# Last layer of a four-layer image kernel: the recurrent state of a pair of images is loaded in seven parts, one per chunk of the pair before, in place of four transfers at once

## What is computed

```python
x = x + _L0_conv_ref(_gn(x), ...)          # attention
x = x + _L1_conv_ref(_gn(x), ...)          # deformable convolution
x = x + _L2_conv_ref(_gn(x), ...)          # diagonal LSTM, left and right
x = x + _L3_conv_ref(_gn(x), ...)          # deformable convolution, adaptive
...
def _diag_lstm(x, w_i2s, b_i2s, w_ih, b_ih, b_hh, k0, k1, b_s2s):
    ...
    _, hs = jax.lax.scan(step, (z, z), xs)            # wd = 2 * w - 1 = 111 steps
    outs = hs.reshape(wd, b, COUT, h).transpose(1, 2, 3, 0)
    return _unshift(outs, w)
left = _diag_lstm(x, *params)
right = jnp.flip(_diag_lstm(jnp.flip(x, 3), *params), 3)
right = jnp.concatenate([jnp.zeros_like(right[:, :, :1, :]), right[:, :, :-1, :]], axis=2)
return left + right
```

## Time and profile before

| | us |
|---|---|
| Median of 3 runs, not profiled | 12763.94 (12756.97 to 12778.16) |
| Span of the profiled execution | 13258.5 |
| POOL busy, of that span | 7518.9 (57%) |
| PE busy | 7451.2 (56%) |
| DVE busy | 6180.1 (47%) |
| Last layer in the profile | 7942 to the end, some 5317 |

### The profile page before, as it was taken

One profiled execution on the slowest core, in us unless ns is written; L12 is line 12 of the kernel. 1 busy time (PEld: TensorE's weight loads), 2 busy tenths in 40 slices (PEclk: granted clock), 3 DMA queues, 4 the chain that ended last, 5 costly groups with the idle time before them and its releaser, 6 DMA issues. The chain is left out here.

```text
span 13258.5 us, 114790 instructions
## 1 busy us (share of the span) xinstructions
PE 7451.2 (56%) x29878; PEld 2708.4 (20%) x29878; DVE 6180.1 (47%) x8631; ACT 4757.6 (36%) x7391; POOL 7518.9 (57%) x7857
## 2 busy tenths in 40 slices
PE   7786776778777676853289992333232323233332
PEld 2222222222222222221123321111111111111111
DVE  1344444444433444445456664454455445545444
ACT  7664554646555454641156661111111111111100
POOL 0375655657565564757500004777777767767776
PEclk9897887889888787876599995565565656555665
DMA  0232232223322222337633337343434343433332
GB/s 9 66 96 87 85 93 80 87 89 96 92 85 79 89 85 86 91 94 172 164 86 81 82 78 139 101 121 101 120 97 119 101 111 98 120 97 101 100 96 90
DMA packets 1169072, 1280.23 MB, mean 97 GB/s; under 512 B 795966, under 2 KB 924414, under 8 KB 1164670
## 3 DMA queue, kind: packets, MB, share of 16 engines
q0 software_dynamic: 338688, 925.30, 23.5%
q1 hardware_dynamic: 815710, 347.84, 11.1%
q10 hardware_dynamic: 14368, 3.21, 0.1%
HBM read 1080.00 MB, written 195.82 MB: 96 GB/s over the span
## 5 line engine op out<-in xcount | busy, mean ns | idle before, releaser
L423 POOL DMA_INDIRECT b_gathered<-table,b_iu x3528 | 3701.6, 1049 | 1929.9 <-issue 1013.0
L423 POOL DMA_INDIRECT d_gathered<-table,d_iu x3528 | 3705.2, 1050 | 1420.4 <-issue 1041.0
L526 PE MATMUL PS<-ident,d_sample 128*128 128x128 f32 (+1 forms) x1960 | 509.6, 424 | 2978.1 <-DVE d_sample L879 2090.9
L504 PE MATMUL PS<-b_key 64*128 64x448 f32 (+1 forms) x5600 | 1516.6, 622 | 448.9 <-ACT b_weights L665 300.1
L665 ACT ACTIVATE b_weights<-PS 128x896 f32<-128x896 f32 (+1 forms) x1400 | 1270.1, 907 | 1287.5 <-remote 882.8
L861 DVE TENSOR_TENSOR d_gathered<-d_gathered,PS 128x2304 f32<-128x2304 f32 x392 | 1000.9, 2553 | 1184.1 <-DMA d_gathered<-table,d_iu 1115.1
L514 PE MATMUL PS<-b_weights,b_values 128*64 128x448 f32 (+1 forms) x5600 | 1462.9, 603 | 123.1 <-issue 73.4
L668 ACT ACTIVATE b_weights<-b_weights 128x896 f32<-128x896 f32 (+1 forms) x1400 | 1332.3, 952 | 44.7
L674 ACT ACTIVATE d_sampleT<-PS 128x512 f32<-128x512 f32 x392 | 233.6, 596 | 2894.4 <-PE PS L526 2000.9
L526 PEld LDWEIGHTS PS<-ident,d_sample 128*128 128x128 f32 (+1 forms) x1960 | 336.0, 205 | 3130.8 <-issue 2721.1
L866 DVE TENSOR_TENSOR b_gathered<-b_gathered,PS 128x1152 f32<-128x1152 f32 x392 | 529.9, 1352 | 819.3 <-DMA b_gathered<-table,b_iu 802.6
(11 more groups left out here) (227 smaller groups left out, 9679.5 us busy)
## 6 DMA issues: line engine op xcount, KB each, us to landing
b_gathered<-table,b_iu POOLq DMA_INDIRECT x3528
d_gathered<-table,d_iu POOLq DMA_INDIRECT x3528
l_x_and_h<-xs SPq DMA_DIRECT2D x224, 224.0 KB, 3.9
hs<-l_hT SPq DMA_DIRECT2D x224, 224.0 KB, 2.8
d_h<-hs SPq DMA_DIRECT2D x32, 1554.0 KB
table<-b_table_rows SPq DMA_DIRECT2D x208, 128.0 KB, 2.0
table<-d_table_rows SPq DMA_DIRECT2D x208, 128.0 KB
xs<-b_key SPq DMA_DIRECT2D x14, 1568.0 KB
```

Of the source, the lines that this page charges most:

```text
L423: pool.indirect_dma_start(GB[:, g, k, :], None, tables[b], bass.IndirectOffsetOnAxis(ap=ix, axis=0)).then_inc(gathered[g], 16)
L504: mm = pe.matmul(PS[0:keys(k), 2 * (k % S_BUFS) + a, 0:CH], KEY[r, 0, k * P:k * P + keys(k)], KEY[r, 0, j * CH:(j + 1) * CH], start=True, ...
L526: mm = pe.transpose(PS[0:n, 5 + 2 * (s // 4), (s % 4) * P:(s % 4 + 1) * P], S[:, t % 2, s * P:s * P + n], K.ident[:, :])
```

## The change

The state is cut along its 111 steps into seven parts: six of 16 steps (`H_PART`), one of 15. `load_h_part` issues the four DMAs (direction, image) of one part. `prepare` still loads whole states with `load_h`, which now issues 28 DMAs for one state. In `body` the load no longer stands between the input's load and the first chunk; each chunk issues its own part ahead of its two `write_group` calls, behind the same wait on `h_used`. DVE waits for 64 x 7 increments per pair in place of 64.

```diff
+H_PART = -(-STEPS // NCH)
...
-            def load_h(i):
+            def load_h_part(i, j, last):
+                steps = STEPS - (NCH - 1) * H_PART if last else H_PART
                 for d in (0, 1):
                     for a in (0, 1):
-                        src = hs[1:SLOTS, d, bass.ds((2 * i + a) * H, H), :].rearrange("t r c -> t (r c)")\
-                            .rearrange("t (c r) -> c t r", c=C)
-                        sp.dma_start(HD[a * C:(a + 1) * C, d, :].rearrange("p (t r) -> p t r", r=H), src)\
-                            .then_inc(h_loaded, 16)
+                        src = hs[bass.ds(1 + j * H_PART, steps), d, bass.ds((2 * i + a) * H, H), :]\
+                            .rearrange("t r c -> t (r c)").rearrange("t (c r) -> c t r", c=C)
+                        to = HD[a * C:(a + 1) * C, d, bass.ds(j * (H_PART * H), steps * H)]
+                        sp.dma_start(to.rearrange("p (t r) -> p t r", r=H), src).then_inc(h_loaded, 16)
+
+            def load_h(i):
+                for j in range(NCH):
+                    load_h_part(i, j, j == NCH - 1)
...
                     load(x, n, X[nb])
-                    if not isinstance(n, int):
-                        wait_apart(sp, h_used, n + 1)
-                        load_h(n + 1)
...
                     elif nxt:
+                        if not isinstance(n, int):
+                            wait_apart(sp, h_used, n + 1)
+                            load_h_part(n + 1, j, last)
                         write_group(n, nb, 2 * j, 0)
...
-                    v.wait_ge(h_loaded, 64 * m + 64)
+                    v.wait_ge(h_loaded, 64 * NCH * (m + 1))
```

## The result

| | median, us | runs | ratio to before, 95% interval |
|---|---|---|---|
| before | 12771.24 (12753.04 to 12780.15) | 20 | |
| changed | 12737.31 (12725.44 to 12749.27) | 20 | 0.9973 (0.9966 to 0.9979) |

The changed kernel is 34 us faster, 0.27%. The forecast time was 12761 with "no difference that can be told" at 0.83 and "faster by over 0.2%" at 0.06; the measured time lies inside the range, but the effect is real, and the sum had given 3 us, at most 6, in that direction.

A forecast was written before the change was run, and what follows sets the result against it. POOL's gather issuing was taken to bound the last layer. A gain of at most 6 us, less 0 to 3 us for small bursts, with SP and start 0, gave 3 us off: 12761 us, range 12730 to 12800.

The forecast's parts named there:

- What bounds the kernel: Last layer: POOL's 3528 gathers, busy and idle ahead, make 5126 of 5317 us, so POOL's issuing sets the pace.
- The burst costs chunk 0 nothing to speak of: Chunk 0 of a pair: the whole-state load costs 1.0 us per pair, so at most 6 us come back.
- rival A: Chunk 0: the state's burst makes it long, so 11.7 us come back six times, 70 us, 12694; chance 0.06.
- Seven small bursts: Each chunk's part delays one block's landing at most 5.5 us, covered by POOL's lead; cost 0 to 3 us.
- a lead of 19.0 us: Last layer: time between a sample's readiness and POOL's earliest need of it, three blocks on; 5.5 us of it used.
- SP's queue: 24 more DMAs per pair on SP, 2.3 us per four at a chunk's head; cost 0, without cover 9.6 us per pair.
- The layer's start: First states, loaded with 28 DMAs each: issues hide behind the transfer, cost 0, bounds 0 and 28 us.
- Rival B: Layer's start: each further DMA adds its issue to the transfer, 28 us slower, 12789; chance 0.06.
- the estimate of 96 us: Layer's start: 2 x 24 further DMAs at 2.0 us fixed cost each, laid end to end, 12857; chance 0.01.
- Rival C: Every chunk: late landings meet POOL where its lead is gone, half the waits cost 50 us, 12811; chance 0.08.
- the 18 waits for a sample: Last layer, first profile: POOL runs out of lead 18 times, for 123.1 us in all, up to 37.3 at once.

The follow-up runs named there:

- loop in parts: Changed kernel, but the layer's start loads two whole states; only the loop loads a part per chunk. Ratio 0.9978, POOL busy 3705.9 us.
- e0_before: The kernel before, unchanged, run and profiled again (the second profile of before). Ratio 1.0001, span 12778.9 us.

## Why the prediction was right and wrong

**What bounds the kernel** was right: POOL's issuing sets the layer's pace, and nearly the whole gain stands in its gathers.

**The burst costs chunk 0 nothing to speak of** was right. It was put at 1.0 us per pair; with the second profile it is 0.2 us (100.2 us with burst, 100.0 without any load), and rival A, 0.06, did not happen. Chunk 0 of pair 6, which loads nothing, takes 101.4 us in that profile, so differences of 1 us between chunks 0 mean nothing. The state itself lands 57 to 59 us behind its first issue there, where the prediction had estimated 51. The long gathers beside the two adds of the state (L741 and L744 before) stayed, as said (5.6 to 6.4 us), and the DMA share just behind normalizing went down, as said: from 1.20 to between 0.43 and 0.47.

**Seven small bursts: the step that failed.** The prediction had the landing at most 5.5 us later, a lead of 19.0 us that absorbs it, and no wait of POOL from it; all of that held, though a part lands 9.6 us behind its first issue in the median, not 7.3, and is issued 20 us into the chunk, not at POOL's first gather of it. It then bounded the cost below by 0. The cost was negative: POOL's busy time fell by 30.5 us (loop in parts). The reason named for the bound was the lead: POOL doesn't wait for DVE, so it can't matter when DVE works. But the same text had, a few paragraphs before, a gather of 5.84 us beside an add with two SBUF inputs. DVE's column add does the same in nearly every block, 0.78 us of the 12.8 on average. I counted this coupling at the two long adds, and not at the 392 short ones, although and the earlier trace rows themselves show gathers of 1.93 us. So "beside other work" had been read as "free", where a second path led from DVE's timing to POOL.

**SP's queue** was right in its outcome: four issues of a part hold SP for 3.6 to 4.7 us, more than the 2.3 us put, and nobody waits.

**The layer's start** was bounded by 0 and +28 us and went to some -4 us. Why 28 DMAs move the same rows sooner than four is not explained by any run here. Rival B of the prediction is wrong in sign. So is the estimate of 96 us from the fixed cost in the Trainium skill (DMA: Bandwidth & Descriptors, "Anatomy of one DMA — SWDGE (gpsimd) path"); the page states that cost for transfers issued from GpSimd, and these go from SP.

**Rival C** rested on the 18 waits for a sample. They belonged to the disturbed execution: the second profile of before has one, the changed kernel one:

```profile
POOL d_gathered L423 <- DVE d_sample L879: 8.5, 1, 8.5
```

```profile
POOL d_gathered L427 <- DVE d_sample L883: 4.8, 1, 4.8
```

A profile 494.6 us longer than the median, with nothing that explains it, should have been taken as a warning on every row about stalls, not only as an offset. It also hid part of the effect: with its stalls its gathers were busy for 3705.2 us, nearly as short as in the changed kernel.

**The chances.** "Faster by over 0.2%" had 0.06, all for a mechanism that isn't there. That the time fell inside the range was luck: the range reached down to 12730 by the runs' own spread and terms that did not occur, and the 34 us came from a term that had been put at 0 to 3 us in the other direction.

## What to carry to other kernels

When an engine sets the pace, don't ask only what it waits for, but what stretches its instructions. Compare the busy time of the same instructions, and look at what runs beside the long ones. Where two engines share something and one follows the other at a fixed distance, they lock, and the phase can be the worst one; here a delay of 0.4 us was worth more than the change of the load, and a delay of 1.1 us was worth less than one of 0.4, so such a delay has to be measured. And an effect like this one should be tested by adding useless work or taking needed work away, since it has the opposite sign from what contention for bandwidth would give.

## What the runs showed of the hardware

- An indirect gather on POOL takes 0.95 us, and one that starts beside a DVE `tensor_tensor` with both inputs in SBUF is held to about its end: 1.86 us beside one of 1.36 us (e0_before), 5.84 us beside one of 5.93 us (the first profile of before). Beside the weighing, whose second input is in PSUM, it is not held.
- An instruction with a single tensor input can hold it too: a gather that starts 0.5 us behind the start of the `tensor_scalar` L749 (1.92 us, 128x3136, SBUF to SBUF) takes 2.23 us, all six times in the loop of e0_before. No run here separates what about that instruction does it.
- A part of 4 x 224 KB in rows of 224 bytes delays the landing of one block's gathers, from 1.8 to 4.6 us behind the last of them in the median. It does not slow POOL's issuing: 190 gathers within 10 us behind a part's issue, and beside none of DVE's holding instructions, take 0.95 us like all others.
- The same 6.2 MB of such rows land some 4 us sooner in 28 DMAs than in four (41.0 to 43.0 against 45.4 to 48.5 us).
